# Graph layer with a recurrent block on one core: another order in the first norm and the last block, and unread TensorE products

## The reference, cut to what matters

```
x = x + gnn(layernorm(x), src, dst)          # h = z @ W + b; mean of h[src] over the edges of each dst
x = x + lstm(layernorm(x)[None])[0]          # one sequence of 3125 nodes as rows... B = 1, T = 3125, H = 256
step:  i = sigmoid(xi + h @ V_i); g = tanh(xg + h @ V_c); o = sigmoid(xo + h @ V_o)
       c = h * c + i * g;  h = o * tanh(c)
```

## Time and profile before

| what | value |
|---|---|
| median of 3 runs | 536.91 us (536.58 to 538.16) |
| the profiled execution | 536.19 us, span 534.3 us |
| PE, PE weight loads | 423.8 us (79%), 367.9 us (69%) |
| DVE, ACT, POOL | 374.0 us (70%), 355.9 us (67%), 213.6 us (40%) |
| mean granted TensorE clock | 0.958 |

### The profile page before, as it was taken

The page is one execution under the profiler, slowest core; times in us unless marked ns, Lnnn a source line. Parts: engine busy times, 40 slices in busy tenths (PEclk is TensorE's granted clock), DMA queues, the critical chain, the costliest instruction groups (busy, mean ns, idle before and its releaser), DMA issues.

```text
span 534.3 us, 15505 instructions
## 1 busy us (share of the span) xinstructions
PE 423.8 (79%) x6151; PEld 367.9 (69%) x6151; DVE 374.0 (70%) x1106; ACT 355.9 (67%) x931; POOL 213.6 (40%) x411
## 2 busy tenths in 40 slices
PE   2167797978899999999999999844776778888880
PEld 2045675767788888888888888734666667777770
DVE  3578799778887767768667343434677768888883
ACT  0235697455776777767767554757788888888880
POOL 4353200152444456346446223231445554544540
PEclk9998999899999999999999999976799999999995
DMA  3334001320000000001000100010000000110111
GB/s 117 138 95 120 0 2 59 104 82 1 24 27 1 1 23 30 1 1 49 2 2 1 48 3 2 1 49 1 2 4 3 3 3 3 52 35 19 52 51 54
DMA packets 9293, 16.92 MB, mean 32 GB/s; under 512 B 1694, under 2 KB 7139, under 8 KB 9214
## 3 DMA queue, kind: packets, MB, share of 16 engines
q1 hardware_dynamic: 7658, 13.32, 7.4%
q10 hardware_dynamic: 676, 1.67, 0.9%
q0 software_dynamic: 880, 0.86, 0.7%
HBM read 6.23 MB, written 9.61 MB: 30 GB/s over the span
## 4 chain that ended last, share of the span: by engine, by line
PE 41%; DVE 28%; ACT 14%; POOL 7%; issue 6%; DMA 2%; DVEq 0%; ACTq 0%
PE bank L1120 10%; PE bank L1195 8%; PE bank L1089 7%; PE bank L1091 7%; DVE ig L1625 4%; DVE hots L1455 4%; DVE c_st L1631 4%; ACT gate L911 3%; ACT tc L925 3%; DVE h L1636 3%; PE bank L1051 3%; POOL rstd L631 2%; PE bank L1137 2%; POOL newton L630 2%; ACT counts L777 2%
## 5 line engine op out<-in xcount | busy, mean ns | idle before, releaser
L1195 PE MATMUL bank<-h,V 128*128 128x63 f16 (+1 forms) x3096 | 108.4, 194 | 36.8 <-DVE h L1636 32.3
L1195 PEld LDWEIGHTS bank<-h,V 128*128 128x128 f16 x3096 | 100.4, 98 | 48.0 <-issue 42.3
L1051 PE MATMUL bank<-hots 128*128 128x125 f16 x625 | 120.7, 221 | 1.1 <-ACT counts L777 0.5
L1455 DVE TENSOR_TENSOR hots<-iota,kp 128x1024 f16<-128x1024 f16 x157 | 105.8, 699 | 21.1 <-PE bank L1051 18.3
L1089 PE MATMUL bank<-h_flat,counts 125*128 125x257 f16 x375 | 98.3, 276 | 0.4 <-ACT counts L777 0.4
L1091 PE MATMUL bank<-h_flat,counts 125*128 125x256 f16 x375 | 97.4, 273 | 0.0
L630 POOL TENSOR_SCALAR newton<-rstd,var_eps 125x1 f32<-125x1 f32 x50 | 33.8, 676 | 129.2 <-DVE rstd L1523 126.7
L777 ACT ACTIVATE counts<-bank 125x500 f16<-125x500 f32 x96 | 55.7, 626 | 20.6 <-PE bank L1051 19.1
L1089 PE MATMUL bank<-h_flat,gx 125*128 125x257 f16 x250 | 68.2, 273 | 0.0
L1091 PE MATMUL bank<-h_flat,gx 125*128 125x256 f16 x250 | 67.4, 270 | 0.0
L657 POOL TENSOR_TENSOR h<-h_flat,h 128x126 f16<-128x126 f32 x82 | 35.9, 438 | 71.0 <-DVE h_flat L1636 71.0
(11 more groups left out here) (161 smaller groups left out, 840.4 us busy)
## 6 DMA issues: line engine op xcount, KB each, us to landing
h_dram<-h_flat SPq DMA_DIRECT2D x1, 3137.2 KB
x_dram<-x_sb SPq DMA_DIRECT2D x5, 625.0 KB
out_dram<-x_sb SPq DMA_DIRECT2D x4, 625.0 KB
x_sb<-in_x_dram SPq DMA_DIRECT2D x3, 625.0 KB
x_sb<-in_x_dram ACTq DMA_DIRECT2D x2, 625.0 KB
out_dram<-x_sb SPq DMA_DIRECT2D x1, 375.0 KB
gx<-in_L_gnn_weight_dram ACTq DMA_DIRECT2D x1, 256.0 KB, 4.1
gx<-in_L_ffn_U_i_dram SPq DMA_DIRECT2D x1, 256.0 KB, 2.8
```

The source lines that it names most:

```text
L1051: nc.tensor.matmul(ps_count[group % 3][:, pos * KEYS:(pos + 1) * KEYS], hots[:, ring, 0, g // 2, :, g % 2], hots[:, ring, 1, g // 2, 0:KEY ...
L1195: mm = nc.tensor.matmul(to[:, (m - m0) * n:(m - m0 + 1) * n], V16[:, v_part, d, m * P:(m + 1) * P], h16[:, h_part, d, c0:c1], start=False, ...
L1455: nc.vector.tensor_tensor(hots[:, k % RING, :, :, :, :].rearrange("p a h n g -> p (a h) n g"), iota[:, :, :].unsqueeze(1).to_broadcast(of) ...
```

## The change

First norm: W's low half and the bias split stand before the second chunk's statistics on DVE; `window_starts` moves from before the loop to turn 3; the six steps of `chunk_deviation` run in one piece in turn 3 of each five (before: spread over turns 2 to 4), and ACT's square root in turn 2; `edge_places` takes two turns (8 and 9) instead of four; `turn_keys` and `copy_keys` move from turn 12 to 10; the one-hots begin in turn 12 instead of 14. Last block: norm, transposes, copies and gates of block 24 move from places 643 to 651 to places 636 to 644, its last root steps from POOL to DVE (`last_root`), turn 25 from place 653 to 650. And PE gets products of `iota` with itself, 256 columns each, into banks that nobody reads: 30 before the first norm, 2 in each of turns 2 to 11 of it, and 12 behind the output products of each of turns 22, 23 and 24.

```diff
-        LAST_AT = {FINISH_AT: (583, 605, 630), NORM_AT: (597, 616, 643), TURN_AT: (600, 618, 643),
-                   HIGH_AT: (601, 619, 645), LOW_AT: (604, 621, 646)}
+        LAST_AT = {FINISH_AT: (583, 605, 630), NORM_AT: (597, 616, 636), TURN_AT: (600, 618, 637),
+                   HIGH_AT: (601, 619, 638), LOW_AT: (604, 621, 640)}
-        LAST_GATES = {PAIRS: (606, 610, 615), PAIRS + 1: (623, 626, 629), PAIRS + 2: (648, 649, 650)}
+        LAST_GATES = {PAIRS: (606, 610, 615), PAIRS + 1: (623, 626, 629), PAIRS + 2: (639, 642, 643)}
-        LAST_TURNS = {21: 609, 22: 620, 23: 631, 24: 637, 25: 653}
+        LAST_TURNS = {21: 609, 22: 620, 23: 631, 24: 637, 25: 650}
-        KEYS_FROM, TURN_KEYS, HOTS_FROM = 8, 12, 14
+        KEYS_FROM, TURN_KEYS, HOTS_FROM = 8, 10, 12
...
-                if j - 1 < BLOCKS:
+                if j - 1 < BLOCKS - 1:
                     root(j - 1, ORDER[j - 1])
...
-                    if j == 2:
-                        deviation(X_CHUNK, 2 * X_CHUNK)
+                    if j % X_CHUNK == 2 and (c + 2) * X_CHUNK <= BLOCKS:
+                        deviation((c + 1) * X_CHUNK, (c + 2) * X_CHUNK)
...
+            def keep_busy(n, to):
+
+                for _ in range(n):
+                    nc.tensor.matmul(to[:, 0:2 * P], iota[:, :, 0], iota[:, :, :].rearrange("p n g -> p (n g)"),
+                                     start=True, stop=True)
+
+            pe.wait_ge(scales_ready, 1)
+            keep_busy(30, bank[4])
             for j in range(BLOCKS + 2):
+                if 2 <= j < HOTS_FROM:
+                    keep_busy(2, bank[4])
...
+                if HIDDEN - 4 < t < HIDDEN:
+                    pe.wait_ge(counted, GROUPS_S * OUTS)
+                    keep_busy(12, bank[2])
...
+            dve.wait_ge(w_hi, 1)
+            dve.wait_ge(consts, 9)
+            nc.vector.scalar_tensor_tensor(out=W16[:, 1, :, :], ...).then_inc(w_split, 1)
+            split_bias()
             for j in range(X_CHUNK, 2 * X_CHUNK):
                 chunk_stats(j)
             chunk_to_root(1)
-            window_starts()
...
-                if c + 1 < BLOCKS // X_CHUNK and 2 <= k:
-                    chunk_deviation(c + 1, 2 * (k - 2))
+                if c + 1 < BLOCKS // X_CHUNK and k == 3:
+                    for part in range(6):
+                        chunk_deviation(c + 1, part)
+                if j == 3:
+                    window_starts()
...
-                if KEYS_FROM <= j < KEYS_FROM + 4:
-                    edge_places(j - KEYS_FROM)
+                if KEYS_FROM <= j < KEYS_FROM + 2:
+                    edge_places(2 * (j - KEYS_FROM))
+                    edge_places(2 * (j - KEYS_FROM) + 1)
...
+            def last_root(j):
+
+                y, t, v = rstd[:, j:j + 1], newton[:, j:j + 1], var_eps[:, j:j + 1]
+                dve.wait_ge(guess_ready, BLOCKS)
+                for three in (3.0, 12.0):
+                    link(nc.vector.tensor_scalar(t, y, v, y, ALU.mult, ALU.mult))
+                    link(nc.vector.tensor_scalar(y, t, -three, y, ALU.add, ALU.mult))
+                link(nc.vector.tensor_scalar(t, y, v, y, ALU.mult, ALU.mult))
+                link(nc.vector.tensor_scalar(t, t, -0.5 / 4096.0, 1.5 / 16.0, ALU.mult, ALU.add))
+                dve.wait_ge(root_ready, BLOCKS - 1)
+                nc.vector.tensor_tensor(y, y, t, ALU.mult).then_inc(root_ready, 1)
+
             def second_norm(j, turn):
+                if turn == BLOCKS - 1:
+                    last_root(j)
```

More of the change, by code:

```diff
@@ L430, in out_group @@
                     i % HOT_WINDOWS == HOT_WINDOWS - 1 or i == WINDOWS - 1)
-        LAST_GATES = {PAIRS: (606, 610, 615), PAIRS + 1: (623, 626, 629), PAIRS + 2: (648, 649, 650)}
-        LAST_GATES_OUT = {PAIRS: (607, 611, 616), PAIRS + 1: (624, 627, 630), PAIRS + 2: (649, 650, 651)}
+        LAST_GATES = {PAIRS: (606, 610, 615), PAIRS + 1: (623, 626, 629), PAIRS + 2: (639, 642, 643)}
+        LAST_GATES_OUT = {PAIRS: (607, 611, 616), PAIRS + 1: (624, 627, 630), PAIRS + 2: (640, 643, 644)}
         def gates_at(w, out=False):
@@ L464, in first_hots @@
         def first_hots(j):
-            return range(max(0, 2 * (j - HOTS_FROM)), max(0, 2 * (j - HOTS_FROM + 1)))
-        assert first_hots(BLOCKS + 3).stop <= OUTS - 1
+            return range(max(0, 2 * (j - HOTS_FROM)), min(max(0, 2 * (j - HOTS_FROM + 1)), OUTS - 2))
         def gates_bank(unit):
@@ L783, in _ @@
             for c in range(BLOCKS // X_CHUNK):
-                if (c + 2) * X_CHUNK <= BLOCKS:
-                    if c > 0:
-                        deviation((c + 1) * X_CHUNK, (c + 2) * X_CHUNK)
                 for j in range(c * X_CHUNK, (c + 1) * X_CHUNK + (2 if (c + 1) * X_CHUNK == BLOCKS else 0)):
@@ L1465, in _ @@
                 chunk_deviation(0, k)
+            dve.wait_ge(w_hi, 1)
+            dve.wait_ge(consts, 9)
+            nc.vector.scalar_tensor_tensor(out=W16[:, 1, :, :],
+                                           in0=w_sb[:, 0:DH * D].rearrange("p (d h) -> p d h", d=DH),
+                                           scalar=w_scale[:, 0:1], in1=W16[:, 0, :, :], op0=ALU.mult,
+                                           op1=ALU.subtract).then_inc(w_split, 1)
+            split_bias()
             for j in range(X_CHUNK, 2 * X_CHUNK):
@@ L1495, in _ @@
                     chunk_stats(j + AHEAD)
-                if c + 1 < BLOCKS // X_CHUNK and 2 <= k:
-                    chunk_deviation(c + 1, 2 * (k - 2) + 1)
                 if 2 * X_CHUNK <= j + AHEAD < BLOCKS and (j + AHEAD) % X_CHUNK == X_CHUNK - 1:
                     chunk_to_root((j + AHEAD) // X_CHUNK)
-                if KEYS_FROM <= j < KEYS_FROM + 4:
-                    edge_places(j - KEYS_FROM)
+                if KEYS_FROM <= j < KEYS_FROM + 2:
+                    edge_places(2 * (j - KEYS_FROM))
+                    edge_places(2 * (j - KEYS_FROM) + 1)
                 for k in first_hots(j):
```

## The result

| | before | after |
|---|---|---|
| median (20 runs each) | 537.15 us | 534.96 us |
| ratio of the two | | 0.9963, interval 0.9946 to 0.9981 |
| profiled execution, span | 536.19, 534.3 us | 534.88, 532.8 us |
| PE busy | 423.8 us | 435.5 us |

A forecast was written before the change was run, and what follows sets the result against it. It took DVE's waits, then ACT and DVE full together to 89.46 us, then PE to 348 us, then engines in turns around block 24. From the 536.91 us median, gains of 3.8 (front) and 1.5 (tail) gave 531.6 us; range 528.3 to 536.0.

The forecast's parts named there:

- the prediction's own sign: Wrong if last one-hots stay above 88, turn 23's cell to turn 25's seed above 11, or an unread product over 0.3 us.
- Front, forecast 3.8: First norm up to the one-hots: gain 4.7 us at full clock or 2.6 at low; 3.8 taken.
- 49.8 or 51.9: Start of the first one-hots at full or low PE clock, 7.9 or 5.8 us earlier than 57.67.
- In turn 8 DVE waits for it: First norm: DVE waits some 3 us for POOL's cast, ending at 40.2, with later blocks' low halves queued behind.
- in PE's waits: First norm: unread pairs of turns 2 to 11, 0.2 to 0.4 us each, lie where PE waits for DVE or edges.
- Behind the one-hots, forecast 3.2 us more work: One-hots start in turn 12 with two more blocks behind: six DVE steps and one small-step series, 2.0 + 1.2 us.
- The middle, forecast untouched: Between the front and block 24: nothing of the change reaches it.
- Tail, forecast 1.5: Block 24 to turn 25's seed: gain 1.9 us at full clock, 0.6 to 1.3 if it falls; 1.5 taken.
- That an unread product costs more than its row: Rival: 24 uncovered products behind turns 22 and 24 cost over 0.11 us each; at 0.45 us, 539.7 us. Chance 0.07.
- The second rival: Clock low through keys and block 24: front gains 2.6, tail loses 2.2 us, total 536.5 us. Chance 0.10.
- The third: Rival: third chunk or gathers land 3 to 4 us later, front gains nothing, 535.4 us. Chance 0.12.
- The first: Rival: clock up everywhere; front 4.7, tail 1.9, turns 26 to 29 some 3.2 us; 527.1 us. Chance 0.08.

The follow-up runs named there:

- early_starts: Changed kernel without the pairs of turns 2 to 11 and with block 10's statistics one turn later on DVE: 531.77 us, 0.9900 of the kernel before.
- front_alone: Kernel before with only the first norm's part of the change, its order and unread products: 536.10 us, 0.9987 of the kernel before.
- order_only: Changed kernel without any unread product: 534.31 us, 0.9937 of the kernel before.
- fill_gaps: Changed kernel with the pairs of turns 2 to 11 replaced by 30, 8 and 14 unread products in turns 3, 9 and 10: 532.68 us, 0.9916.
- joined_spread: `joined` with the root steps of the last two chunks spread between DVE's other work as before the change: 526.56 us, 0.9809 of the kernel before.
- no_pairs: Changed kernel without the two unread products in each of turns 2 to 11: 534.72 us, 0.9966 of the kernel before.
- joined_w12: `joined` with 20 more unread products at place 12 of the middle: 526.80 us, 0.9815 of the kernel before.
- tail_alone: Kernel before with only block 24's new places, last root on DVE and 12 unread products behind each of turns 22 to 24: 533.87 us, 0.9940.
- joined: `early_starts` with unread products at 30 ahead, 14, 8, 12 in turns 3, 9, 10, and 12 behind turn 23 alone: 527.13 us, 0.9811.
- no_thirty: `early_starts` without the 30 unread products ahead of the first norm: 532.55 us, 0.9918 of the kernel before.

## Why the prediction was right or wrong

**Sign and range** held (534.96 in 528.3 to 536.0). **The sum** was 5.3 us, measured 2.0 (1.0 to 2.9). By the prediction's own sign it is wrong in the front: the last one-hots were to end before 88, and they ended at 89.1. In the two profiled executions it divides so:

- *Front, forecast 3.8, found 0.35 at the weights' maximum (89.39 to 89.04), and -0.8 at block 0.* The step that failed is the instant of the first one-hots, "49.8 or 51.9": the 3.8 meant 50.7 and they came at 53.61, 2.9 us late. (a) 0.8: the third chunk landed later than I took, 25.26, and the search ended at 28.95 instead of 27.9, the cast at 41.03 instead of 40.2. That this wait is on the path was shown by `early_starts`. It lay in the text as a bound, not in the sum. (b) 1.75: "In turn 8 DVE waits for it, with the low halves ... queued behind": DVE did not wait for the cast; it came late. I had put the pairs of turns 2 to 11 "in PE's waits", but from turn 3 to turn 7 PE has no wait, and it works at 1.2 GHz until 39 us. I looked for the fall of the clock in turns 9 and 10 and not in turns 2 and 3, where PE idles for 3.1 and 4.0 us. DVE's wait for the square root (1.65 us) follows from that, and with it a small step meets POOL's cast (0.46 us more). The pairs aren't the whole reason: `front_alone`, with the pairs, has none of (b), and `order_only`, without them, has 1.53. What both follow is the time at which the clock rose. (c) 0.35 between first pass and one-hots: the low clock at the keys. The two levels forecast for this stretch, 9.6 and 11.7 us, were both measured; the 10.5 that the 3.8 meant was a middle, and the changed kernel had 10.83. `fill_gaps` shows the price in the ten transposes, 1.06 us.
- In `front_alone` the one-hots are 2.5 us late without (b): the cast ends at 41.40 instead of 40.2, and 11.7 us follow instead of 10.5. So the failed step doesn't hang on one execution; how it divides does.
- *Behind the one-hots, forecast 3.2 us more work, found 3.7* (35.43 instead of 31.72; the same program as before took 31.72 to 32.46). `joined_spread` fits the excess: the steps of two chunks in one piece cost 1.1 us against the spread ones, and I had left out that price for the later chunk.
- *The middle, forecast untouched, found -1.1 in this execution*: 13.85 instead of 12.72 us from the maximum to block 0. The clock was low for 6.8 us there and for 3.4 before. `front_alone` had 13.6, `no_pairs` 12.69 with the same program there. Of the 14 kernels nine had 12.7, four (the changed one, `front_alone`, `fill_gaps`, `joined_spread`) 13.6 to 14.0, and `joined_w12` 11.1. Whether the change makes the longer one more frequent isn't shown.
- *Tail, forecast 1.5, found 1.6*: 363.48 - 362.68 = 0.80 on a start that was 0.78 later. The dozen behind turn 22 cost 1.30 (forecast 1.3). The interval to turn 25's seed was 8.89 (forecast 8.6; 0.3 by the root on DVE, 1.7 us for seven steps, not 1.4). The state of turn 23 came behind the norm, as written. The dozen behind turn 24 held the two units up for 1.3 us, as written, but the seed by only 0.8 to 1.0 (8.68 in `tail_alone` against 7.89 and 7.64). The clock fell behind turn 23 and was back for the gates; that cost 0.2 us at most (8.68 in `tail_alone`, where it never fell), not the 0.6 to 1.3 that made me take 1.5 instead of 1.9.
- *Behind the seed, forecast untouched, found 0.7*: 534.3 - 363.48 = 170.8 us before, 532.8 - 362.68 = 170.1 after. In `front_alone`, with the same program there, it was 168.6. This is the spread between executions and no gain of the change; that the parts (0.35, -1.1, 1.6, 0.7) add up to the 1.5 us between the two spans, and nearly to the 2.0 measured, is in part luck.
- *The rivals.* That an unread product costs more than its row is refuted: the dozens took 1.47 us at 2.4 GHz and 2.77 at 1.2, 0.11 and 0.21 each. The second rival was right for the clock at the keys and wrong for the tail. The third had the right place, the chunk ahead of the search, but a third of the size. The first did not occur.

The Trainium skill's rule for transposes (TensorE: Matmul & The Clock Gate, Part 4: the full clock doesn't engage in that mode) made another time of the keys. The rows here speak against its reach: ten transposes behind busy work took 1.23 us in `fill_gaps` and `joined`, 2.29 in the changed kernel at 0.50. They run at the clock that is granted; whether transposes alone would lift it, no run here shows. The Trainium skill (same page, Part 1) has the engine in its low state by default. This is borne out by `no_thirty`: every six products take 1.54 us up to 47.03 although PEclk reads 1.00.

## What to carry to other kernels

Unread products paid here only in a wait of PE that was about as long as they are, directly ahead of work on the path: the dozen behind turn 23 gave 0.7 to 1.5 us, the same dozen ahead of work that was ready cost 0.8 to 1.3, and two in each turn cost 0.43 us a turn once PE was the bound. One trace of each kernel isn't enough to divide a gain of a few microseconds: four executions of the same first norm lay 1.6 us apart. Where an edit moves a wait on one engine, work out which engine idles through it and at which clock it comes back, and price that engine's next turns at the low clock. A chain that starts with a transfer should have nothing ahead of it on its engine that waits for another transfer.

## What the runs showed of the hardware

- The clock granted to PE is worth microseconds and differs between executions of one program. In the 20 executions of the changed kernel its mean lay between 0.943 and 0.958, the span between 534.7 and 530.9 us.
- PEclk can read 1.00 while PE runs at half speed, up to the first change that the column shows: in `no_thirty` it does so in every slice from 14 to 60 us, and six products take 1.54 us up to 47.03 and 0.88 from 50.81 on. The time of a known group of products tells the clock.
- A small DVE step that met POOL's cast of 125x1280 lasted until the cast was done: 0.62, 1.24 and 1.20 us instead of 0.17 in the changed kernel, `order_only` and `no_thirty`, ending 0.02 to 0.04 us behind the cast.
- Seven dependent steps on one column on DVE took 1.8 us (353.70 to 355.47): 0.27 us each where two operands are per-partition scalars, 0.21 with one, 0.15 to 0.16 for the others. I had counted 0.2 for each.
